# Mixing matrices of a conditioned mixture-of-experts block, formed by TensorE products instead of VectorE sums

## The reference

```python
h = gelu(cond @ W0 + b0);  h = gelu(h @ W1 + b1)          # 64 x 128
att = softmax(h @ W2 + b2)                                # 64 x 8
agg_w = einsum('bk,koi->boi', att, weight)                # one 32 x 32 matrix for each sample
agg_b = att @ bias_k                                      # 64 x 32
xt = einsum('boi,bih->boh', agg_w, x) + agg_b[:, :, None] # 2048 token rows of 512
out = x + moe_ffn(xt)   # router (16 experts, top 2 of the top 2 groups of 4), experts, shared expert
```

## Time and profile before

| | us |
|---|---|
| median of 3 runs | 257.58 |
| the three runs | 257.49, 257.58, 259.15 |
| the profiled execution, its own time | 259.11 |
| its span, first to last instruction | 257.2 |

### The profile page before, as it was taken

One profiled execution on the slowest core, in us unless ns is written; L12 is line 12 of the kernel. 1 busy time (PEld: TensorE's weight loads), 2 busy tenths in 40 slices (PEclk: granted clock), 3 DMA queues, 4 the chain that ended last, 5 costly groups with the idle time before them and its releaser, 6 DMA issues.

```text
span 257.2 us, 3960 instructions
## 1 busy us (share of the span) xinstructions
PE 241.2 (94%) x1092; PEld 163.7 (64%) x1093; DVE 148.5 (58%) x314; ACT 78.7 (31%) x169; POOL 111.3 (43%) x135
## 2 busy tenths in 40 slices
PE   7947989899999988999999999999999999999994
PEld 6815767688877444667777777777777754444441
DVE  0599698838979979333333333334444420099895
ACT  2223345521317400233333333333333331100400
POOL 7782355421011056366666666666666331000170
PEclk9999799999999999999999999999999999999999
DMA  7998387689053946974445444455544222999965
GB/s 219 341 415 317 148 300 261 255 282 412 23 226 118 417 202 182 324 270 164 164 163 164 165 130 158 133 173 173 166 165 157 89 92 78 345 388 387 396 256 186
DMA packets 20698, 57.90 MB, mean 225 GB/s; under 512 B 2533, under 2 KB 2533, under 8 KB 20428
## 3 DMA queue, kind: packets, MB, share of 16 engines
q1 hardware_dynamic: 15084, 39.89, 42.2%
q0 software_dynamic: 5600, 17.83, 20.8%
HBM read 40.94 MB, written 17.30 MB: 226 GB/s over the span
## 4 chain that ended last, share of the span: by engine, by line
PE 78%; DVE 17%; issue 2%; DMA 1%; ACT 0%; DVEq 0%
PE psum L546 69%; PE psum L690 6%; DVE xT L1173 3%; DVE r L943 3%; DVE xT L912 2%; DVE xT L938 2%; PE psum L589 2%; DVE xT L953 2%; PE psum L703 2%; DMA xT<-cond_pack 1%; DVE x_early L912 1%; DVE mix_bias L940 1%; DVE xt_sb L1173 1%; DVE xt_sb L912 0%; DVE code_f L1107 0%
## 5 line engine op out<-in xcount | busy, mean ns | idle before, releaser
L546 PE MATMUL psum<-wexp,r 128*128 x272 | 68.4, 381 | 0.3 <-DVE r L1129 0.3
L546 PEld LDWEIGHTS psum<-wexp,r 128*128 128x128 f32 x272 | 48.5, 190 | 22.8 <-issue 16.8
L912 DVE TENSOR_TENSOR r<-psum,ebias 128x256 f32<-128x256 f32 x34 | 14.4, 425 | 65.0 <-PE psum L546 63.4
L487 POOL DMA_INDIRECT expert_rows<-late_region,to_row x33 | 33.4, 1011 | 33.6 <-ACT late_region L855 28.7
L481 POOL DMA_INDIRECT late_region<-xt_rows,from_row x36 | 35.3, 981 | 17.3 <-issue 10.8
L546 PE MATMUL psum<-wexp,xt_sb 128*128 x68 | 34.8, 594 | 0.0
L849 ACT ACTIVATE r<-r 128x128 f32<-128x128 f32 x34 | 10.5, 310 | 57.6 <-DVE r L912 47.6
L546 PE MATMUL psum<-xT,shared_sb 128*128 128x512 f32 x64 | 28.0, 593 | 0.0
L855 ACT ACTIVATE late_region<-psum 128x512 f32<-128x512 f32 x34 | 20.3, 598 | 13.9 <-issue 7.7
L1129 DVE COPY r<-psum 128x512 f32<-128x512 f32 x36 | 24.5, 680 | 0.0
L690 PE MATMUL psum<-ident,late_region 128*128 128x128 f32 x144 | 21.6, 273 | 1.0 <-DMA late_region<-xt_rows,from_row 1.0
(11 more groups left out here) (175 smaller groups left out, 309.8 us busy)
## 6 DMA issues: line engine op xcount, KB each, us to landing
wexp<-expert_pack SPq DMA_DIRECT2D x16, 768.0 KB, 4.5
wexp<-expert_rows SPq DMA_DIRECT2D x8, 1024.0 KB, 13.1
xt_rows<-xt_sb SPq DMA_DIRECT2D x16, 256.0 KB, 2.2
x_early<-x SPq DMA_DIRECT2D x2, 1024.0 KB, 7.9
late_region<-x SPq DMA_DIRECT2D x2, 1024.0 KB, 12.5
ebias<-expert_bias SPq DMA_DIRECT2D x1, 2048.0 KB, 7.1
out_dram<-x_early SPq DMA_DIRECT2D x8, 256.0 KB, 9.3
shared_sb<-shared_pack SPq DMA_DIRECT2D x1, 1536.0 KB, 16.3
```

Source lines behind the costliest of these rows:

```text
L487: nc.gpsimd.indirect_dma_start(out=y_dram[:, :], out_offset=bass.IndirectOffsetOnAxis(ap=rows_of.bitcast(U32), axis=0), in_=y_sb[:, slot, ...
L546: return nc.tensor.matmul(dst, lhsT, rhs, start=start, stop=stop)
L912: return nc.vector.tensor_tensor(dst, a, b, op)
```

## The change

The host now packs the kernels as `mix_pack`, an array of 8 rows: for each of 33 outputs o (32 rows of the kernel and the bias), the 32 input values of that row four times over, 128 values. It goes by a transfer of its own on SyncE's queue, second in order, into `mix_w`, 8 partitions of `xT` (132 KB). The kernel part of `cond_pack` is gone (602 columns of float32 become 338), and its samples are in their own order.

On the chip the softmax ends with a plain 64 x 8 product. TensorE transposes it to 8 x 64, three warming products follow, VectorE copies the transposed attention to SBUF, and 33 products of 8 rows, one for each o, each with 128 columns of weights against 64 columns (the samples), write all 64 matrices into PSUM banks 4 to 7 and the biases into bank 3. VectorE then copies: four bias copies of 32 partitions by 16, and for tiles 0 to 3, 4 to 7 and 8 to 15 four copies each onto the block diagonal. All 16 copies stand ahead of the first copy into `xT`, and the tile loop holds no `mix` any more. TensorE's first router product waits for all of them, because it writes bank 4.

The masks, their GpSimd instructions and the product with `is_block` are gone, and of the two runs of 8 warming products the second becomes a run of 3 in another place.

```diff
@@ shapes
-        mix_w = early(P, KMIX * (IN_C + 1)).rearrange("p (k o) -> p k o", k=KMIX)
+        mix_w = xT[0:KMIX, :, :, :].rearrange("k g c n -> k (g c n)")[:, 1024:1024 + (IN_C + 1) * P].rearrange(
+            "k (o m) -> k o m", m=P)
+        attT = early(KMIX, BS)
+        mixes = psum[:, 4:8, :].rearrange("p g n -> p (g n)").rearrange("p (o t r) -> p r t o", t=NT, r=BPT)
+        mixes_bias = psum[:, 3, 0:BS].rearrange("p (t r) -> p r t", r=BPT)
-        MIXES = [(0, 1), (1, 2)] + [(t, t + 2) for t in range(2, NT, 2)]
+        MIXES = [(0, GT), (GT, 2 * GT), (2 * GT, NT)]
@@ sync
             sp.dma_start(cond_in, cond_pack).then_inc(cond_loaded, 16)
+            sp.dma_start(mix_w, mix_pack).then_inc(mix_loaded, 16)
@@ gpsimd
-            link(nc.gpsimd.memset(is_tile, 0.0))
-            for r in range(BPT):
-                link(nc.gpsimd.affine_select(out=is_tile, ...))
-            link(nc.gpsimd.memset(is_block, 1.0))
-            link(nc.gpsimd.affine_select(out=is_block, ...))
-            nc.gpsimd.affine_select(out=is_block, ...).then_inc(masks_ready, 1)
@@ tensor
             keep_warm(8)
-            pe.wait_ge(masks_ready, 1)
             pe.wait_ge(dve_cond, 2)
-            mm(psum[:, 5, 0:NT * KMIX], is_block.rearrange("b r i -> b (r i)"),
-               att_spread.rearrange("b t k -> b (t k)")).then_inc(pe_cond, 1)
-            keep_warm(8)
+            nc.tensor.transpose(psum[0:KMIX, 5, 0:BS], att, ident[0:BS, 0:BS]).then_inc(pe_cond, 1)
+            keep_warm(3)
+            pe.wait_ge(mix_loaded, 16)
+            pe.wait_ge(dve_cond, 3)
+            for o in range(IN_C + 1):
+                last = mm(psum[:, 4 + o // 8, (o % 8) * BS:(o % 8 + 1) * BS] if o < IN_C else psum[:, 3, 0:BS],
+                          mix_w[:, o, :], attT)
+            last.then_inc(pe_cond, 1)
@@ tensor, the tile loop, at the first router product
                         pe.wait_ge(router_loaded, 16)
+                        pe.wait_ge(mix_copied, len(MIXES))
@@ vector
-            V.scalar_tensor_tensor(out=att_spread, in0=att_e..., scalar=att_rec, in1=is_tile..., ...)
+            V.tensor_scalar(att, att_e, att_rec, None, ALU.mult).then_inc(dve_cond, 1)
             dve.wait_ge(pe_cond, 4)
+            V.tensor_copy(attT, psum[0:KMIX, 5, 0:BS]).then_inc(dve_cond, 1)
             dve.wait_ge(blocks_zeroed, 1)
-            def mix(first, end): ...
-            for step in range(3):
-                mix(*MIXES[step])
+            dve.wait_ge(pe_cond, 5)
+            for r in range(BPT):
+                rows = slice(r * IN_C, (r + 1) * IN_C)
+                V.tensor_copy(mix_bias[rows, :], mixes_bias[rows, r])
+            for first, end in MIXES:
+                for r in range(BPT):
+                    rows = slice(r * IN_C, (r + 1) * IN_C)
+                    last = V.tensor_copy(mixT[rows, first:end, rows], mixes[rows, r, first:end, :])
+                last.then_inc(mix_copied, 1)
             for t in range(NT):
                 ...
-                if t % 2 == 0 and 3 + t // 2 < len(MIXES):
-                    mix(*MIXES[3 + t // 2])
```

More of the change, by code:

```diff
@@ L17, with adaln_moe_ffn @@
 TAKEN = -3.0e30
-def adaln_moe_ffn(nc, x, cond_pack, router_pack, shared_pack, expert_pack, expert_bias, down_bias, out):
+def adaln_moe_ffn(nc, x, cond_pack, mix_pack, router_pack, shared_pack, expert_pack, expert_bias, down_bias, out):
     BS, IN_C, DIM = x.shape
@@ L70, in adaln_moe_ffn @@
             x_split, w_split = x_split_sb[:, :, :, :, :], w_split_sb[:, :, :]
+        psum = ctx.enter_context(nc.psum_tensor("psum", [P, 8, 512], F32))
         PRODUCTS = ((0, 0), (0, 1), (1, 0))
@@ L194, in adaln_moe_ffn @@
         to_slot = sb("to_slot", [P, RING], I32)
-        psum = ctx.enter_context(nc.psum_tensor("psum", [P, 8, 512], F32))
         cond_loaded = sem("cond_loaded")
@@ L209, in adaln_moe_ffn @@
         ident_ready = sem("ident_ready")
-        masks_ready = sem("masks_ready")
+        mix_loaded = sem("mix_loaded")
         blocks_zeroed = sem("blocks_zeroed")
@@ L392, in _ @@
                                     base=0, pattern=[[-1, P]], channel_multiplier=1).then_inc(ident_ready, 1)
-            link(nc.gpsimd.memset(is_tile, 0.0))
-            for r in range(BPT):
-                link(nc.gpsimd.affine_select(out=is_tile, in_=is_tile, compare_op=ALU.not_equal, fill=1.0,
-                                             base=-NT * r, pattern=[[-1, NT]], channel_multiplier=1))
-            link(nc.gpsimd.memset(is_block, 1.0))
[L399 to L403, removed]
             nc.gpsimd.memset(r1[:, :], 0.0).then_inc(blocks_zeroed, 1)
@@ L1198 @@
     cond, b2 = np.asarray(inputs["cond_128"]), a["b2"]
-    _, out_c, in_c, _ = a["weight"].shape
     chunks, dim = a["ffn_router_w"].shape[0] // P, a["ffn_router_w"].shape[0]
@@ L1212, in everywhere @@
         return np.broadcast_to(v, (P, v.size))
-    mix = np.concatenate([a["weight"][..., 0].transpose(2, 0, 1), a["bias_k"].T[:, :, None]], axis=2)
-    blocks = P // out_c
-    by_place = cond.reshape(-1, blocks, cond.shape[1]).transpose(1, 0, 2).reshape(cond.shape)
+    mix = np.concatenate([a["weight"][..., 0], a["bias_k"][:, None, :]], axis=1)
+    mix = np.tile(mix, (1, 1, P // mix.shape[2]))
     arrays = {
         "x": a["x"],
-        "cond_pack": np.concatenate([by_place.T, a["W0"], a["W1"], a["W2"], a["b0"][:, None], a["b1"][:, None],
-                                     everywhere(b2), np.tile(mix.reshape(in_c, -1), (blocks, 1))], axis=1),
+        "cond_pack": np.concatenate([cond.T, a["W0"], a["W1"], a["W2"], a["b0"][:, None], a["b1"][:, None],
+                                     everywhere(b2)], axis=1),
+        "mix_pack": mix,
         "router_pack": np.concatenate([rows(a["ffn_router_w"]), everywhere(a["ffn_router_b"]),
```

## The result

The changed kernel takes **262.4 us** (median of 6 runs, 260.92 to 263.71); the kernel before, run beside it, 259.02 (6 runs). The ratio is **1.0152 [1.0106, 1.0198]**: slower, by 1.5%. Two runs of before at a mean granted clock near 0.97 (263.28 and 264.98 us) are left out of the ratio, and the median of the other four is 258.2; no trace shows where their clock is missing. The forecast was 255.8 with a range from 254.0 to 262.0. All six runs of the changed kernel had a mean granted clock of 0.964 to 0.974. The profiled one is the fastest of them (260.92 us, 0.974), and its page says where its clock is missing.

A forecast was written before the change was run, and what follows sets the result against it. TensorE was taken as the bound, so what counts is its start on the shared expert: tile 0 at 20.91 plus 35.38 gives 56.29 against 58.11, 1.8 us gained, 257.58 to 255.8 us; range 254.0 to 262.0.

The forecast's parts named there:

- the first rival: In the 33 products, half clock: each of 66 instructions costs 0.108 us more, all 7.1, giving 262.9 us; chance 0.20.
- over 1% slower: Threshold within the half-clock case: from 41 of the 66 product instructions at the lower clock level, the kernel is that slow.
- the second rival: Behind the products, ahead of tile 0, the clock falls once: at most 1.7 us lost, giving 257.5 us; chance 0.15.
- the cheap price: VectorE's PSUM copies ahead of tile 0: 0.285 us for 128 elements, four 1.14 us.
- the dear price: VectorE's strided PSUM copies at 0.38 us each, delaying tile 0 by 0.4 us and the first router product by 0.8.
- the row on line 1045: Earlier profile row cited for VectorE's strided PSUM copies, against the price of 0.38 us a copy.
- the 0.121 that I took: Pitch in us of the 66 weight loads in the 33 products, taken from neighbours against 16 columns.
- the third rival: In the products, 8-row loads no longer hidden behind the stream: 0.054 us more each, 3.6 in all, 259.4; chance 0.10.
- The fourth: In the products, load pitch falls with the rows: 8 rows in half the time, 4.0 us less, 251.8; chance 0.08.
- my bound of 0.25: At the first product, the smaller `cond_pack` gains between 0 and 0.25 us, TensorE's idle for it; 0.2 taken.

The follow-up runs named there:

- e3: The changed kernel with a full 128-row warming product behind every third of the 33 products, 11 more: 272.25 us, ratio 1.0538 to the kernel before.
- e2: The changed kernel with its products streaming 128 columns instead of 64, still over 8 rows: 261.93 us, ratio 1.0135 to the kernel before.
- e12: e6 with zeros in rows 8 to 127 of the kernel matrices: 255.36 us, ratio 0.9876 to the kernel before.
- e4: The changed kernel with the 33 products spread over four 32-row groups, 8 rows used of each: 252.98 us, ratio 0.979 to the kernel before.
- e6: e1 with seven warming products added behind the 33 products, while VectorE copies: 254.8 us, ratio 0.9895 to the kernel before.
- e7: e4 with seven warming products added behind the 33 products: 252.11 us, ratio 0.9765 to the kernel before.
- e9: e7 with each product over all 32 rows of its group, kernels four times over, attention divided by 4: 250.92 us, ratio 0.9739 to the kernel before.
- e11: e9 with zeros in rows 8 to 31 of the kernels and the attention not divided by 4: 250.93 us, ratio 0.9703 to the kernel before.
- e10: e9 with ScalarE copying two of four blocks, bias copies behind the first four tiles' blocks, three warming products: 251.62 us, ratio 0.9753 to the kernel before.
- e1: The changed kernel with its 33 products over 128 rows instead of 8, kernels and attention repeated 16 times: 258.26 us, ratio 0.9992 to the kernel before.

## Why the prediction was wrong

**What failed** is one sentence, the argument against the first rival: "it held from 29 to 58 with pauses, and here TensorE is never idle in the stretch." TensorE wasn't idle (2.00 of 2.00), and the clock fell all the same. I saw that "no row shows such a stream" over 8 rows, had two facts for the 29 to 58 stretch (pauses, products of 128 rows) and weighed only the first. So the sum held the clock's cost in the products at nothing; it was 3.8 us. That rival had 0.20; it came at part strength. About 35 of the 66 instructions ran at the lower level, and its price for one (+0.108) was right: 0.215 against 0.11 here, and six loads cost 1.35 instead of 0.75 in e3, 0.10 each. The sum put the point of "over 1% slower" at 41 such instructions; it was passed with fewer because the second rival came on top.

**The second rival** (the fall behind the products, 0.15, at most 1.7 us) also came true: 1.6 us from tile 0 to tile 3. The two were priced as exclusive, and they add: a clock that is down when the pause begins isn't brought back by the pause. That sum wasn't made. From 56.29 to 60.46 are 4.2 us: +3.1 in the products (11.36 against 8.27), +1.6 to tile 3, +0.2 in the copies, -0.7 in the start.

**What the stages don't explain.** The median is 6.6 us above the forecast (262.4 against 255.8), the profiled execution 3.6 above the 257.3 forecast for it. The other 3.0 are two steps of 1.5 from a profiled execution to a median: before's took 1.5 more than the median that the forecast started from (259.11 against 257.58), the changed kernel's is the fastest of six. The second step may be another fall of the clock. e2's profiled execution has a mean clock of 0.964, as two of the changed kernel's six have, and its trace shows a second hole from 61 to 64.4 us, in which the 72 shared-expert instructions take 18.19 us instead of 16.61. For the changed kernel itself no trace shows it. That 262.4 lies so near the 262.9 of the first rival at full strength is chance: just over half of that rival came, and the rest is the second rival and these steps.

**What held.** The rest is best read in e12, where the clock stays up. Tile 0 at 19.86 and the shared expert at 55.27 lie 35.41 apart (forecast 35.38); tile 0 to tile 3 took 4.59 (forecast 4.58); the steps are 2.19. The copies of 128 elements cost 0.287 (forecast 0.285, the cheap price; the dear one was 0.38), those of 256 elements 0.42, the bias copies 0.72 together (forecast 0.62). So the row on line 1045 was the right neighbour. The rule of the Trainium skill, page SBUF — State Buffer, section Door 1: The DMA port swizzle, on PSUM's lines of 8 bytes is about matmuls; carried over to VectorE it would have given the dear price, and at a stride of 256 bytes the trace doesn't bear that out.

**Pitch.** 7.48/66 = 0.113 at full clock with 128 rows (e12), below the 0.121 that I took and at the end that the earlier trace rows gives; the stage was forecast 0.7 us too long (8.27 against 7.59). With 8 rows the pitch at full clock is the same: 30 loads in 3.32 us in the changed kernel as in e12, and 30 in 3.26 in e2, with twice the columns. So loads stay hidden behind the stream, and the third rival, which wanted 0.175, falls. The fourth, a pitch that falls with the rows, falls too. The fall to 0.032 in e4 comes from the groups, not from the size.

**The start** was 10.08 instead of 10.73. The smaller `cond_pack` gave 0.46 at the first product (3.46 against 3.92), above my bound of 0.25, which was the idle of the matmuls, whose ends are modelled. The weight loads, which went first, were idle for longer. This is their row in before, which I didn't read:

```profile
3.92 0.50 PEld L546 LDWEIGHTS psum<-xT 128*128 128x128 f32 x2 [0.54 <-DMA xT<-cond_pack]
```

The head also varies from one execution to the next. e6 and e12 have the same head, and their products begin at 9.17 and 10.20: eight warming loads from 3.68 took 1.53 in the one and 1.83 in the other, the four behind them 0.53 and 0.97. That is the step from the slower pitch to the faster one, sooner in e6, though the clock column reads 1.00 in both. A difference of 1 us between the starts of two single profiles can be that alone.

**What the change is worth by itself**: e6 and e12, the change with both clock losses removed, give 0.9895 [0.9831, 0.9959] and 0.9876 [0.9781, 0.9971], where the forecast had 255.8/257.58 = 0.993. The mechanism stood, and the clock took some 2.6% of the time (1.015 against 0.989), more than twice the gain.

**Still open**: why e3's full products didn't help; whether a row count between 8 and 32 would do (not run), or zeros in the streamed rows too; and a second fall in e2, e4 and e7, at 61, 52 and 51 us, as the shared expert begins or shortly after, behind router products that name all 128 rows. It costs e7 some 1.6 us in its 72 shared-expert instructions (18.20 against 16.61), most of the distance between its profile and e9's. Two of e7's four executions have a mean clock of 0.986, like the profiled one, and two of 0.993; the latter are 1.5 us faster. Stretches of e7 and, behind it, of e2:

```profile
52.00:56.00 4.00, 4.00 (x14) 3.17 (x14) 3.34 (x8) 0.42 (x1) 0.99 (x3) 0.73 0.74 280
...
60.00:62.00 2.00, 2.00 (x10) 1.73 (x10) 1.27 (x3) 0.07 (x1) 1.05 (x3) 0.75 0.80 301
62.00:64.00 2.00, 2.00 (x6) 1.54 (x6) 1.51 (x4) 0.35 (x1) 0.00 (x0) 0.50 0.91 375
64.00:66.00 2.00, 2.00 (x10) 1.62 (x9) 1.86 (x6) 0.00 (x0) 0.00 (x0) 0.90 0.94 385
```

So the row count decides the fall in this stage, and isn't all that moves the clock.

## What to carry to other kernels

Before moving arithmetic from another engine to TensorE, ask how much of the array each product fills, not only whether the engine stays busy: where the sum runs over 8 terms, pad the weights with zeros to 32 rows, repeat the streamed operand beside them as e11 does, and deal the products out over the four row groups. The padding added no time to the products (2.22 us in e7 and in e11), and the two together took the stage from 11.3 to 2.2 us. Cover the pause that follows with products into an unused bank, and read the granted clock of both stretches; price a fall and the pause behind it as adding up. When a stage ahead of saturated DMA engines gets faster, look at when the stores land before counting the gain (e10).

## What the runs showed of the hardware

- The clock falls under a TensorE that is busy throughout: 0.50 for products of 8 rows, 64 or 128 columns; 1.00 for the same of 128 rows, with or without zeros in the weights, and of 32 rows in four groups; 0.80 and then 0.50 behind the products of 8 rows in four groups (e7). Products at the lower level: 11.3 us instead of 7.5.
- A pause of 2.17 us behind full products was followed by a fall (e1, 0.51 at 20 to 22 us); with all but 0.56 us of it covered there was none (e6). One of 2.21 us in the kernel before wasn't followed by one for 5.9 us.
- Float32 products spread over four row groups issue every 0.032 us, each with a load of 128 columns against 64; in one group, or over all 128 rows, every 0.11.
- ScalarE copies 32 partitions of 128 elements from PSUM in 0.268 us and of 256 in 0.376 (e10); VectorE took 0.281 and 0.415 beside it, 0.287 and 0.421 alone.
